# Last stage summed on TensorE, the mixer's first and last batch spread over all PSUM banks, the second batch's expert rows added inside the mixer

## The reference

```
x = x + ga * attention(layernorm(x) * (1 + ca) + sa)
x = x + gb * experts(layernorm(x) * (1 + cb) + sb)
```

```
h  = gelu(ragged_dot(xs, w1, tokens_per_expert))      # rows sorted by expert
ys = ragged_dot(h, w2, tokens_per_expert) * flat_w[order][:, None]
out = zeros.at[tok].add(ys) + bias                    # two experts a row
```

```
src = rmsnorm(x + gqa(x)) ; logits = src @ gate_w ; two experts of eight a row, with a capacity
src = src + sum over k of out_padded[gather_idx] * w_topk
return rmsnorm(src)                                   # times gb, added to x
```

## Time and profile before

| what | value |
|---|---|
| median of three runs | 3484.88 us |
| the profiled execution | 3496.94 us, of which the span is 3495.2 |
| PE, DVE, ACT, POOL busy over the span | 3089.8, 2152.1, 1665.8, 1166.9 us |
| routed experts' last additions | 1254.8 to 1266.0 us |
| mixer | 1268.8 to about 2810 us |
| layer 1's experts | 2813 to about 3351 us |
| last stage | 3355.9 to 3495.2 us |

### The profile page before, as it was taken

How to read it: one execution, slowest core, us unless ns; L and a number is a source line. 1 busy time by engine, 2 the same in 40 slices (tenths; PEclk the granted TensorE clock), 3 DMA queues, 4 the chain that set the end, 5 groups by cost and what they waited for, 6 DMA issues and landing times. The chain is left out here.

```text
span 3495.2 us, 57784 instructions
## 1 busy us (share of the span) xinstructions
PE 3089.8 (88%) x18233; PEld 1906.4 (55%) x18233; DVE 2152.1 (62%) x5625; ACT 1665.8 (48%) x3734; POOL 1166.9 (33%) x1536
## 2 busy tenths in 40 slices
PE   6999999999989946999999999999998779999930
PEld 3667677676756723344444444444443368888820
DVE  7777777777742223777777777777777422222269
ACT  2565555556431122666666666666665411111134
POOL 2132322323251132334444444444432222222245
PEclk8999999999999976999999999999999889999965
DMA  7010101101028810222222222222222057777754
GB/s 256 26 70 35 69 35 62 42 37 67 36 96 284 300 54 28 64 58 70 72 73 69 73 72 73 69 70 75 73 71 72 24 188 231 235 236 238 222 165 147
DMA packets 249505, 370.22 MB, mean 106 GB/s; under 512 B 25071, under 2 KB 184891, under 8 KB 247200
## 3 DMA queue, kind: packets, MB, share of 16 engines
q1 hardware_dynamic: 233888, 329.57, 29.4%
q0 software_dynamic: 14832, 34.57, 2.8%
q10 hardware_dynamic: 544, 3.15, 0.2%
HBM read 242.18 MB, written 130.34 MB: 107 GB/s over the span
## 5 line engine op out<-in xcount | busy, mean ns | idle before, releaser
L2314 ACT ACTIVATE pT<-psum 128x512 f32<-128x512 f32 x1024 | 599.3, 599 | 364.8 <-PE psum L3027 340.7
L2569 DVE TENSOR_REDUCE negmax<-psum 128x2 f32<-128x1024 f32 x512 | 625.0, 1221 | 219.1 <-PE psum L3000 203.3
L3027 PE MATMUL psum<-q_stack,k_stack 99*128 99x512 bf16 x1024 | 378.6, 383 | 19.7 <-issue 9.2
L3000 PE MATMUL psum<-k_stack,q_stack 96*128 96x512 bf16 x1024 | 310.3, 384 | 59.0 <-DVE negmax L2569 42.6
L955 ACT ACTIVATE probs<-probs,negmax 128x256 f32<-128x256 f32 x512 | 252.8, 495 | 132.0 <-DVE negmax L1045 128.3
L3343 ACT ACTIVATE actT_x<-psum 128x512 f32<-128x512 f32 x142 | 84.8, 597 | 441.8 <-PE psum L3409 441.8
L3373 DVE COPY ye<-psum 128x512 f32<-128x512 f32 x71 | 49.1, 692 | 399.6 <-PE psum L3421 399.6
L3039 PE MATMUL psum<-pT,v_tile 128*32 128x512 f32 x2048 | 274.4, 608 | 1.0 <-ACT pT L2314 1.0
L3331 POOL DMA_INDIRECT chosen_out<-ye,place x142 | 139.7, 984 | 398.1 <-DVE ye L3373 239.6
L3409 PE MATMUL psum<-xT_x,w_x 128*128 128x256 f32 x1136 | 257.9, 380 | 0.0
L3421 PE MATMUL psum<-w_x,actT_x 128*128 128x256 f32 x1136 | 256.6, 379 | 0.0
(11 more groups left out here) (376 smaller groups left out, 5912.7 us busy)
## 6 DMA issues: line engine op xcount, KB each, us to landing
w_x<-in_L_ffn_w_dram SPq DMA_DIRECT2D x142, 512.0 KB, 4.2
w_e<-in_L_ffn_w_dram SPq DMA_DIRECT2D x46, 1024.0 KB, 7.1
q_stacks<-q_part SPq DMA_DIRECT2D x192, 128.0 KB
q_stack<-q_stacks SPq DMA_DIRECT2D x64, 384.0 KB, 3.6
padded<-w_e SPq DMA_DIRECT2D x32, 645.0 KB, 5.6
xe<-padded SPq DMA_DIRECT2D x71, 258.0 KB
gate_rows<-mods SPq DMA_DIRECT2D x66, 256.0 KB, 3.3
chosen_out<-w_e SPq DMA_DIRECT2D x16, 1024.0 KB, 7.6
```

The lines of the kernel that those rows point to most:

```text
L2314: act.activation(pT[:, 4 * (s % 2) + r, :], bank(m, 2 + n % 2), ACT.Exp, scale=float(DHQ) ** -0.5)\
L2569: dve.tensor_reduce(negmax[:, p // 2, h:h + 2], m.psum[:, 0:2, :], AX.X, ALU.max, negate=True)\
L3000: mm = pe.matmul(bank(m, j), q_stack[0:K_SCORE, h, t * P:(t + 1) * P], k_stack[0:K_SCORE, g, :], start=True, stop=True)
L3027: pe.matmul(bank(m, 2 + n % 2), k_stack[:, g, kc * P:(kc + 1) * P], q_stack[:, REP * g + r, :], start=True, stop=True).then_inc(sT_done, 1)
```

## The change

It has four parts.

1. **Second batch.** The end of the routed experts handles only the first batch (NT instead of NTL tiles), with its sums in PSUM. The second batch's rows are loaded as the mixer starts, into tiles that are idle then; ScalarE weighs the first rows after its first small steps, and VectorE does the rest (`add_second_batch`).
2. **Start of the mixer.** The first batch is normalised on VectorE, the memset stands after that, and ScalarE waits for two early constants only.
3. **Banks.** The first batch's linear attention, second normalisation and queries and keys, and the last batch's final steps, take another bank for each step (tables FIRST and LAST), and the waits for the previous content go. The first twelve pairs of score products of the first batch alternate between banks 0, 1 and 2, 3.
4. **Last stage.** TensorE adds src and the weighed first rows by products with the identity, in three pairs of banks; VectorE's sum stays in PSUM, and so does the root (banks 6 and 7). GpSimd keeps only the addition to x.

The diff, cut to its core:

```diff
@@ routed_experts_block
-        acc = sb("acc_e", [P, NTL, D])
+        acc = sb("acc_e", [P, NT, D])
...
-            for t in range(NTL):
+            for t in range(NT):
                 act.wait_ge(got_in[t // 2], 16)
-                act.activation(acc[:, t, :], got[:, t, 0, :], ACT.Copy, ...
+                act.activation(bank(m, t)[:, 0:D], got[:, t, 0, :], ACT.Copy, ...
...
-                step(dve.scalar_tensor_tensor(out=acc[:, t, :], in0=got[:, t, 1, :],
+                step(dve.scalar_tensor_tensor(out=bank(m, t)[:, 0:D], in0=got[:, t, 1, :],
...
-                dve.tensor_tensor(acc[:, t, :], acc[:, t, :], rows2[:, t // NT, 0, :], ALU.mult)...
+                dve.tensor_tensor(acc[:, t, :], bank(m, t)[:, 0:D], rows2[:, 0, 0, :], ALU.mult)...
@@ mixer_block
+        got1 = pT[:, 0:4, :].rearrange("p a (k d) -> p a k d", k=TOPK)
+        acc1 = oraw[:, 0:2, :].rearrange("p a (u d) -> p (a u) d", u=2)
+        gate1 = resid[:, 0, :]
...
+        FIRST = dict(hidden=(5, 0), query=(1, 2), key_value=(3, 4, 7, 6), numerator=(0, 1, 2, 3), o1=(4, 7),
+                     project1=(5, 0), hidden2=(6, 7), query_key=(6, 7, 4))
+        LAST = dict(weighed=(0, 1, 2, 3), o2=(4, 5), project2=(6, 7), src=(0, 1))
+        def lb(b, product, i):
+            return bank(m, FIRST[product][i] if is_first(b) else LB)
...
+        def max_bank(b, n):
+            return 2 * (n % 2) if is_first(b) and n < 12 else 0
...
+            sp.dma_start(got1.rearrange("p t k d -> p t (k d)"), chosen_out0[S * TOPK:2 * S * TOPK, :] ...
+            sp.dma_start(gate1, mods_dram[0, 1, 2, :].partition_broadcast(P)).then_inc(gate1_in, 16)
             for b in range(-3, 2):
...
             def normalise_first(b):
+                if is_first(b):
+                    return
...
-            for b in range(-3, 2):
+            body(-3, 1, lambda k: k == 3)
+            act.wait_ge(consts, 9)
+            act.wait_ge(got1_in, 16)
+            for t in range(NT):
+                j = (NT + t) * TOPK
+                act.activation(acc1[:, t, :], got1[:, t, 0, :], ACT.Copy, scale=m.route_w0[:, j:j + 1])...
+            for b in range(-2, 2):
...
-            dve.memset(k_stack[K_SCORE:K_FULL, :, :], 1.0).then_inc(consts, 1)
...
             body(-3, 1, lambda k: k == 3)
-            dve.wait_ge(consts, 12)
+            normalise_first_batch()
+            dve.memset(k_stack[K_SCORE:K_FULL, :, :], 1.0).then_inc(ones_ready, 1)
+            add_second_batch()
+            dve.wait_ge(consts, 9)
...
             def keys_values(b, t):
-                if t:
-                    pe.wait_ge(v1_ready, b * NT + t)
-                else:
-                    pe.wait_ge(q_read, b * C + C)
+                if not is_first(b):
+                    if t:
+                        pe.wait_ge(v1_ready, b * NT + t)
+                    else:
+                        pe.wait_ge(q_read, b * C + C)
...
             def project2(b, j):
-                if j:
+                if j == 0:
+                    pe.wait_ge(o2T_ready, b * 2 + 2)
+                elif not is_last(b):
                     pe.wait_ge(r_ready, b * 2 + 1)
...
@@ combine_block
+        def y(b, t):
+            return bank(m, 2 * (b % 3) + t // 2)[:, (t % 2) * D:(t % 2 + 1) * D]
+        def root(b):
+            return bank(m, 6 + b % 2)[:, 0:NT]
...
-            def add_src(b):
-                pool.wait_ge(first_ready, (b + 1) * NT)
-                first = got[:, b % GB, :, 0, :]
-                pool.tensor_tensor(first, first, m.src_all[:, b, :, :], ALU.add).then_inc(src_added, 1)
...
+        @block.tensor
+        def _(pe):
+            for b in range(B):
+                if b >= 3:
+                    pe.wait_ge(z_ready, (b - 2) * NT)
+                for i in range(2):
+                    pe.matmul(bank(m, 2 * (b % 3) + i), m.ident[:, :],
+                              m.src_all[:, b, 2 * i:2 * i + 2, :]..., start=True, stop=False)
+                for i in range(2):
+                    pe.wait_ge(first_ready, b * NT + 2 * i + 2)
+                    pe.matmul(bank(m, 2 * (b % 3) + i), m.ident[:, :], got[:, b % GB, 2 * i:2 * i + 2, 0, :],
+                              start=False, stop=True).then_inc(sum_done, 1)
...
-                    act.wait_ge(y_ready, b * NT + t + 1)
-                    act.activation(square[:, t, :], y[:, b % YB, t, :], ACT.Square, scale=1.0 / 16.0,
+                    act.wait_ge(y_ready, b * NT + 2 * (t // 2) + 2)
+                    act.activation(square[:, t, :], y(b, t), ACT.Square, scale=1.0 / 16.0,
...
-                dve.wait_ge(src_added, b + 1)
                 for t in range(NT):
+                    dve.wait_ge(sum_done, 2 * b + t // 2 + 1)
...
-                    dve.scalar_tensor_tensor(out=y[:, b % YB, t, :], in0=y[:, b % YB, t, :], scalar=rms[...],
+                    dve.scalar_tensor_tensor(out=z[:, b % YB, t, :], in0=y(b, t), scalar=rms[:, u, t:t + 1],
```

More of the change, by code:

```diff
@@ L1493, in routed_experts_block @@
         sent = [sem(f"b_sent{u}") for u in range(2)]
-        got_in = [sem(f"b_got_in{j}") for j in range(NTL // 2)]
+        got_in = [sem(f"b_got_in{j}") for j in range(NT // 2)]
         second_ready = sem("b_second_ready")
@@ L1533, in _ @@
                 sp.wait_ge(sent[u], 16 * ((NTILE0 + 1 - u) // 2))
-            for j in range(NTL // 2):
+            for j in range(NT // 2):
                 sp.dma_start(got[:, 2 * j:2 * j + 2, :, :].rearrange("p t k d -> p t (k d)"),
@@ L2479, in first_newton, with normalise_first_batch, add_second_batch @@
                 step.close()
+            def normalise_first_batch():
+                dve.wait_ge(stats1, 1)
+                for t in range(NT):
+                    dve.tensor_scalar(xn[:, t, :], x_tile(0, t), mv1[:, t, 0:1], rstd1[:, t:t + 1], ALU.subtract,
+                                      ALU.mult).then_inc(xn_ready, 1)
+            def add_second_batch():
+                step = Steps(dve, sum1_s, 0, 0)
+                dve.wait_ge(gate1_in, 16)
+                dve.wait_ge(got1_in, 16)
+                for t in range(NT):
+                    j = (NT + t) * TOPK + 1
+                    dve.wait_ge(first1_ready, t + 1)
+                    step(dve.scalar_tensor_tensor(out=acc1[:, t, :], in0=got1[:, t, 1, :],
+                                                  scalar=m.route_w0[:, j:j + 1], in1=acc1[:, t, :], op0=ALU.mult,
+                                                  op1=ALU.add))
+                    step.settle()
+                    step(dve.tensor_tensor(acc1[:, t, :], acc1[:, t, :], gate1, ALU.mult))
+                    step.settle()
+                    step(dve.tensor_tensor(x_tile(1, t), x_tile(1, t), acc1[:, t, :], ALU.add))
+                step.settle()
             def second_stats(b, j):
@@ L2590, in normalise @@
                 dve.wait_ge(ot_done, b * NT + t + 1)
-                o = bank(m, RB).rearrange("p (h w) -> p h w", w=VW)
+                o = rb(b, "weighed", t).rearrange("p (h w) -> p h w", w=VW)
                 dve.reciprocal(osum[:, t, :], o[:, :, DHQ]).then_inc(osum_s, 1)
@@ L2967, in queries_keys @@
                     pe.wait_ge(h2_ready, b * C + C)
-                else:
+                elif not is_first(b):
                     if i == 2:
```

206 lines of the change are left out of this document (112 added, 94 removed).

## The result

The changed kernel takes 3381.57 us (median of four runs, 3379.94 to 3384.06), the kernel before 3484.64 (3482.41 to 3486.28). The ratio is 0.9705, 95% interval 0.9688 to 0.9722: 103 us less. The direction was forecast; the time is 24 us under the forecast of 3406 and 8 under the lower end of the range.

A forecast was written before the change was run, and what follows sets the result against it. The last stage was taken as bound by VectorE standing still while GpSimd works, the mixer's first and last batch by hand-offs. Gains of 5.6 + 5.2 + 6.0 + 5.6 + 1.6 + 4 + 5.2 + 45.7 = 78.9 gave 3406 us, range 3390 to 3432.

The forecast's parts named there:

- VectorE standing still: Last stage: VectorE's instructions with two SBUF operands wait under GpSimd's additions; four at L3560 take 5.84 us instead of 1.67.
- the blocked engine: Rival, last stage: PSUM operands don't free VectorE of GpSimd, 2.3 us more a batch, 3438 us; chance 0.04.
- the low clock: Rival, last stage: TensorE's clock stays low or half low, 3422 to 3438 us; chance 0.15.
- 4.6 us a batch: Last stage: a batch falls from 7.93 to 4.6 us; the stage gains 45.7 us.
- the head: From the routed experts' end through the mixer's first twelve maxima: gains of 5.6, 5.2, 6.0, 5.6, 1.6 and 4 us.
- the last batch: Mixer's last batch: transposes 2.3 and 0.7, projection 1.1, router transposes 1.1 us; gain 5.2 us.
- the rival of slower mixed transfers: Rival, last stage: mixed loads and stores slower than loads alone, 5.3 us a batch, 3416 us; chance 0.07.
- the first batch's numerators and projections: Mixer's first batch, division and projection: numerators 3.8, second transpose 0.7, second projection 1.1 us; gain 5.6 us.
- queries, keys and values: Mixer's first batch, first query product to Gram product: 23.9 us become 17.9, gain 6.0; 0.4 at the low clock throughout.
- the stretch up to the maxima: Mixer's first batch, second normalisation and keys: 0.8 and 0.8, together 1.6 us gained; the second batch's own products keep their time.
- the end of the routed experts: Four tiles with sums in PSUM instead of eight, stride 0.92 us instead of 1.20; gain 5.6 us.
- the 12 us between the two: Kernel before: profiled execution 3496.94 us, median 3484.88, 12.06 lower; this difference was carried over to the forecast median.

The follow-up runs named there:

- experiment 5: Changed kernel, last stage's VectorE weighing reading one operand from SBUF instead of PSUM: 5.82 us a batch, 3410.93 us in all (one run).
- experiment 6: Changed kernel with a further 128x320 GpSimd addition of two SBUF tensors a batch in the last stage: 3.71 us a batch, 3378.95 us in all (one run).
- experiment 7: Changed kernel without ScalarE's logarithm in the last stage: 3.71 us a batch, 3380.04 us in all (one run).
- experiment 8: Changed kernel with one of VectorE's small steps in place of three in the last stage: 3.61 us a batch, 3376.49 us in all (one run).
- experiment 9: Changed kernel without ScalarE's logarithm and two of VectorE's three small steps: 3.43 us a batch, the last three batches 3.93 apart; 3383.32 us in all (one run).
- experiment 10: Changed kernel with four row buffers instead of five in the last stage: 3.71 us a batch, later 3.90 to 3.95; 3383.20 us in all (one run).
- experiment 4: Changed kernel with the second batch's expert rows added in the routed block again, not in the mixer: median 3388.51 us, ratio 0.9707.
- experiment 3: Changed kernel with one bank per phase again, waits put back, in the mixer's first and last batch: 3412.02 us, ratio 0.9784.
- experiment 1: The kernel before, unchanged, in a second profiled execution: 3492.57 us, 1354.3 us in the mixer's middle.

## Why the prediction was right or wrong

**Right: VectorE standing still.** The reading of the earlier trace rows, that a PSUM operand frees VectorE from GpSimd, is shown by experiments 5 and 6, and the blocked engine falls away as a rival. So does the low clock, by the 1.00 in the windows of the stage.

**Wrong: 4.6 us a batch in the last stage.** This is the step that failed: "Four engines within 15% of each other hand work on, so I take 4.6 us a batch". I had the engines at 3.9 to 4.1, 3.75, 3.4 and the transfers at 4.05, and put half a microsecond on top for which no row spoke. (These are three engines and the transfers, and they lie up to 20% apart, not 15%. The sum for the stage's start also comes to 3376.3 and not 3376.6, which changes little.) The runs show no margin at all: the slowest queue sets the batch, VectorE's 3.71 us, then ScalarE's 3.61, then TensorE's 3.43, each seen in its turn when the one above it was made shorter (experiments 7 to 9). The engines work on different batches, with three pairs of PSUM banks between them, and after the second batch no bracket stands in front of any of VectorE's weighings. That the buffers are the reason was not tested. VectorE itself came out lower than my 3.9, since four instructions of 0.48 us start 0.39 us apart. Fourteen batches of 0.89 us are 12.5 us. The other 2.9 of the stage are its start (the second batch's small steps 19.2 us after the load, not 20.7) and the last batches, where VectorE has no weighing left to do. Together the stage gave 15.4 us more than forecast, the largest part of the miss; the head and the last batch gave 6.4 and 5.0 more. My range had left out all parts at their best bounds, and that is the side on which the time fell.

**Half wrong: the transfers.** The size was right, 3.93 against 4.05 us for load and store, and the rival of slower mixed transfers did not come true. But even at 3.93 they did not bind in 16 batches: five loads are issued ahead, and each batch eats only 0.2 us of that lead. I treated the rate as a bound for each batch, without counting how long the lead lasts. Experiments 9 and 10 show where it ends.

**Too small: the last batch (5.2, measured 10.2) and the head (28.0, measured 34.4).** The hand-offs came as forecast: the four transposes of the last batch gave 2.7 us (2.3 forecast), the first batch's numerators and projections 6.7 (5.6). What I left out is the clock: 3.6 us in the projections of the last batch, in the two executions compared. In four of ten executions of the new last batch 1.6 to 2.1 us of that are missing, so the 10.2 are at the upper end: the averages are 26.6 us (four old) and 18.2 (ten new), a gain of 8.4. I had used the clock as a condition for queries, keys and values and nowhere else. The head's largest miss is the stretch up to the maxima, 2.8 us. The second batch's transposes and queries, which I had left as they were, gave 1.6 (one query group at the full clock instead of the low one), the key product 3.2 instead of 0.8, and 1.3 were lost behind it, most of them in a longer wait for the load of `k_stack` (9.30 us against 8.40). TensorE's timeline of after:

```profile
1316.00 1.04 PE L3039 MATMUL psum<-ident,xn 128*128 128x128 f32 x8
...
1318.52 1.98 PE L3056 MATMUL psum<-h2T,qw 128*128 128x512 f32 x4 [1.49 <-ACT h2T L2309]
...
1320.34 1.88 PE L3052 MATMUL psum<-h2T,kvw 128*128 128x512 f32 x4
```

The key product stands 1.8 us behind the query product; before it was 5.0 (1346.44 to 1351.44). Of the 3.2 saved, 1.5 are the clock (the query product took 3.44 us there, 1.98 here) and the rest a wait for VectorE that I had put at 0.8. The 1 us by which queries, keys and values came out better than forecast (7.0 against 6.0) is partly luck: the queries took 5.6 us and not 6.8, while the wait before the Gram product was 4.3 and not the 3.0 of before. By experiment 3 the banks, with the clock that goes with them, are worth 20 us in the head (24 at most against the other executions) and 6 to 10 in the last batch.

**Right: the move of the second batch.** For the end of the routed experts 5.6 us were forecast and 6.2 measured (experiment 4), with ScalarE giving back 0.5.

**Right for the median, wrong for the profiled execution: the 12 us between the two.** They belong to the one profiled execution of before, so taking them off was right for the median: the medians differ by 103 us, 24 more than my sum of 78.9, and those 24 are the whole miss of the time. The forecast of 3418.0 for the profiled execution was wrong by them, since the changed kernel's profiled execution (3381.57) is its median. Most of the 12 us sat in the mixer's middle, 9.3 us longer there than in the changed kernel and 6.0 longer than in experiment 1, and the 106 us gained outside the middle are close to the 103 of the medians.

## What to carry to other kernels

Where several engines work on different batches with buffers between them, as in this stage, take the longest queue as the batch's length and add nothing, unless a row shows a wait. For a transfer that is slower than the engines, count how many batches its lead lasts before calling it a bound. And wherever a gap in front of TensorE goes, price its products at both clocks and let the range hold both: in the last batch the clock was worth up to 3.6 us against 1.0 for the hand-off, and in four executions of ten 1.6 to 2.1 us less than that. One profiled execution on each side can't tell such a stretch; several can.

## What the runs showed of the hardware

That PSUM is written in place by VectorE at 483 ns for 128 x 256, the same as with the second operand in SBUF (484), had no row before. Four such instructions in a row take 1.57 us from start to start of the next group, less than four times their duration.

GpSimd's 128x1024 addition takes 2.36 us when all of VectorE's instructions have an operand in PSUM, and 2.52 us in experiment 5, where the weighings read two SBUF tensors (the earlier trace rows had 2.52 as well).

Loads and stores mixed moved 385 and 400 GB/s in the two full windows, no less than the loads alone in the earlier trace rows (388).
